# A four-stage transformer block on one core: expert products with gate and up weights stationary, and the order of the first attention units of layer 1

## The reference

```python
# experts: E=16, top 2, 128 hidden units each
p = sigmoid(x @ gate_w.T); p = p / sum(p)
w, idx = top_k(p, 2); w = w / sum(w)
gate, up = split(x @ gate_up_proj[e])        # [256, 2*128] for expert e
y_e = (silu(gate) * up) @ down_proj[e]       # [128, 256]
out = sum over the two chosen experts of w_e * y_e
# layer 1, per head: rope on q and k, alibi, 30*tanh(s/30), causal softmax, context, Wo
```

## Time and profile before

| | |
|---|---|
| median of 3 runs | 534.26 us (533.25 to 538.05) |
| profiled execution | 533.59 us |
| its span, first to last instruction | 531.1 us |
| mean granted TensorE clock | 0.974 |
| TensorE busy, the page | 497.8 us, 94% of the span |
| expert stage, first up record to last scatter | 221.1 to 275.8 us |

### The profile page before, as it was taken

How to read it: one execution, slowest core, us unless ns; L and a number is a source line. 1 busy time by engine, 2 the same in 40 slices (tenths; PEclk the granted TensorE clock), 3 DMA queues, 4 the chain that set the end, 5 groups by cost and what they waited for, 6 DMA issues and landing times.

```text
span 531.1 us, 10729 instructions
## 1 busy us (share of the span) xinstructions
PE 497.8 (94%) x3592; PEld 434.7 (82%) x3592; DVE 380.4 (72%) x833; ACT 339.7 (64%) x761; POOL 294.0 (55%) x289
## 2 busy tenths in 40 slices
PE   8999999999999996899958979999999999999994
PEld 7668888888888785688836869999999999999883
DVE  4798888888883275655537897779857985588556
ACT  5756777777766646344324776778766876676663
POOL 5757677767764136255551676776554664465330
PEclk9999999999999999899987988999999999999998
DMA  8939999940000672455564000000000000000001
GB/s 270 398 85 383 314 331 318 322 151 0 0 1 1 225 295 81 114 156 162 181 216 171 0 1 2 1 0 2 1 2 1 1 2 0 2 1 1 0 22 60
DMA packets 17756, 56.78 MB, mean 107 GB/s; under 512 B 2628, under 2 KB 12362, under 8 KB 15914
## 3 DMA queue, kind: packets, MB, share of 16 engines
q1 hardware_dynamic: 14960, 49.81, 27.5%
q0 software_dynamic: 2752, 6.40, 3.6%
HBM read 49.19 MB, written 28.45 MB: 146 GB/s over the span
## 4 chain that ended last, share of the span: by engine, by line
PE 78%; DVE 7%; ACT 5%; issue 3%; DMA 3%; POOL 2%; SPq 0%; DVEq 0%; POOLq 0%; ACTq 0%
PE bank L443 10%; PE bank L445 10%; PE bank L444 10%; PE bank L991 5%; PE bank L586 5%; PE bank L508 4%; PE bank L611 3%; PE bank L1008 3%; PE bank L588 2%; PE bank L735 2%; PE bank L720 2%; PE bank L722 2%; PE bank L721 2%; PE bank L622 2%; PE bank L702 2%
## 5 line engine op out<-in xcount | busy, mean ns | idle before, releaser
L1100 ACT ACTIVATE probs<-bank,neg_max,q_scale 128x256 f32<-128x256 f32 (+1 forms) x128 | 63.7, 507 | 39.1 <-DVE neg_max L1770 39.1
L1986 POOL TENSOR_TENSOR probs<-probs,inv_sum 128x512 f32<-128x512 f32 x64 | 51.5, 826 | 44.1 <-DVE inv_sum L1778 44.1
L2019 POOL TENSOR_TENSOR exps<-exps,tables 128x256 f32<-128x256 f32 x32 | 24.7, 771 | 75.2 <-ACT exps L1210 75.0
L1210 ACT ACTIVATE exps<-bank 128x768 f32<-128x768 f32 x32 | 25.9, 808 | 41.3 <-PE bank L702 41.3
L1590 DVE TENSOR_TENSOR q_lo<-q_sum,q_hi 128x512 fp32r<-128x512 f32 x32 | 28.8, 899 | 29.0 <-ACT q_hi L1164 28.6
L2006 POOL TENSOR_TENSOR swapped<-swapped,tables 128x512 f32<-128x512 f32 x32 | 43.4, 1359 | 5.2 <-ACT swapped L1131 5.1
L2115 POOL DMA_INDIRECT y_rows<-y_slot,dest x31 | 29.7, 959 | 30.0 <-issue 18.2
L1756 DVE TENSOR_TENSOR swapped<-bank,tables 32x512 f32<-32x512 f32 x64 | 44.4, 693 | 1.4
L1978 POOL TENSOR_TENSOR qT<-qT,swapped 128x512 f32<-128x512 f32 x32 | 40.8, 1274 | 6.1 <-DVE swapped L1756 6.1
L443 PE MATMUL bank<-x,wq_hi 128*128 128x256 f32 x128 | 38.6, 301 | 0.1
L586 PE MATMUL bank<-keysT,qT 128*128 128x256 f32 x128 | 38.2, 380 | 0.0
(11 more groups left out here) (281 smaller groups left out, 1766.6 us busy)
## 6 DMA issues: line engine op xcount, KB each, us to landing
slots<-in_c_unused SPq DMA_DIRECT2D x20, 1036.0 KB, 35.5
gu_all<-in_gate_up SPq DMA_DIRECT2D x4, 1024.0 KB, 7.8
xg<-slots SPq DMA_DIRECT2D x31, 129.5 KB, 2.2
wvo_raw<-in_wvo SPq DMA_DIRECT2D x1, 2560.0 KB, 18.4
dn_all<-in_down SPq DMA_DIRECT2D x1, 2048.0 KB, 7.7
wq_full<-in_Wq SPq DMA_DIRECT2D x1, 2048.0 KB, 17.8
wo_raw<-in_Wo SPq DMA_DIRECT2D x1, 2048.0 KB
wqk_raw<-in_wqk SPq DMA_DIRECT2D x1, 1536.0 KB, 9.9
```

Of the source, the lines that this page charges most:

```text
L1100: ins = act.activation(probs[:, par, h, c0:c1], bank[:, 2 * par + h, c0:c1], ACT.Exp, bias=neg_max[:, par, i:i + 1], scale=q_scale[:, b, t ...
L1986: ins = pool.tensor_tensor(some, some, inv, ALU.mult)
```

## The change

**Experts.** ScalarE gets a new step `take_weights(k)`: it reads the expert's number of block k into a register and copies that expert's 128 x 512 gate and up weights from `gu_all` to one of two fixed places (`GU = 2`) in `gu_block`. `up(k)` then takes these as the stationary operand and moves the block's 128 rows, in four matmuls of 128 columns, so that its result has hidden units on partitions, gate in columns 0 to 127 and up in 128 to 255. The product of silu and up is then already what `down` needs: `turn_act` and `copy_act` are gone, and the loops have one stage fewer. `gate_block(k)` writes `actT`, and `down(k-1)` follows `up(k)`. The first two `take_weights` stand ahead of ACT's first `copy_block`; later ones follow `silu`, two blocks ahead.

**Layer 1.** In units n = 1 to 3 DVE's `context_norm(n-1)` and (n = 2, 3) `context_lo(n-2)` follow `query_cos(n+3)` directly, ahead of `query_lo`, `keys_sum` and `query_sum`; in units n = 2 and 3 ACT's `context_hi` stands ahead of `act_query_hi` and exp. The two tiles of `normalise(1, 1)` are taken apart: the first stands at the head of unit 1, the second behind `query_lo(3)`.

```diff
@@ -273,7 +274,8 @@
     eps, minus_half = table_probe[:, 19:20], table_probe[:, 17:19]
     idx_f = x_rows[:, :, D:D + TOP]
     xT_f32 = q_sum
-    gated, act_tok = (swapped[:, i, 0:2 * FF].rearrange("p (i n) -> p i n", i=2) for i in range(2))
+    gu_block = q_sum[:].rearrange("p g (c f) -> p g c f", c=KD)
+    gated = swapped[:, 0, 0:2 * P].rearrange("p (i n) -> p i n", i=2)
     wk_hi, wk_lo = w_hi, w_lo
     slots = nc.dram_tensor("slots", (REGIONS * REGION, W), F32, kind="Internal").ap()
     y_rows = nc.dram_tensor("y_rows", (TOP * (B * T + KINDS * REGION), D), F32, kind="Internal").ap()
...
@@ -981,26 +980,22 @@
                 mm = pe.transpose(bank[:, turned(k), c * P:c * P + P], xg[:, k % XG, c * P:c * P + P], ident[:])
             mm.then_inc(mo["xgT_done"], 1)
 
-        def up(k, experts):
+        def up(k):
             pe.wait_ge(mo["xgT_copied"], k + 1)
+            pe.wait_ge(mo["gu_copied"], k + 1)
             if k >= 2:
                 pe.wait_ge(mo["act_ready"], k - 1)
-            for c in range(KD):
-                for i, e in enumerate(experts):
-                    rows = slice(ROWS * i, ROWS * i + ROWS)
-                    mm = pe.matmul(bank[rows, up_bank(k), 0:2 * FF], xgT[:, k % 2, c, rows],
-                                   gu_all[:, bass.ds(e, 1), c, :].rearrange("p e f -> p (e f)"),
-                                   start=c == 0, stop=c == KD - 1, skip_group_check=True)
+            for i in range(PER_STEP):
+                rows = slice(ROWS * i, ROWS * i + ROWS)
+                for half in range(2):
+                    dst = bank[:, up_bank(k), half * P + ROWS * i:half * P + ROWS * i + ROWS]
+                    for c in range(KD):
+                        mm = pe.matmul(dst, gu_block[:, k % GU, c, half * FF:half * FF + FF], xgT[:, k % 2, c, rows], start=c == 0, stop=c == KD - 1,
+                                       skip_group_check=True)
             mm.then_inc(mo["up_done"], 1)
 
-        def turn_act(k):
+        def down(k, experts):
             pe.wait_ge(mo["act_ready"], k + 1)
-            if k >= 2:
-                pe.wait_ge(mo["actT_copied"], k - 1)
-            pe.transpose(bank[:, actT_bank(k), 0:P], act_tok[:, k % 2, :], ident[:]).then_inc(mo["actT_done"], 1)
-
-        def down(k, experts):
-            pe.wait_ge(mo["actT_copied"], k + 1)
             if k >= 2:
                 pe.wait_ge(mo["y_copied"], k - 1)
             for i, e in enumerate(experts):
...
@@ -1016,18 +1011,16 @@
             pe.wait_ge(x_or_expert_in[j], 32)
         turn_block(0)
         experts_of = {}
-        for i in range(STEPS + 2):
+        for i in range(STEPS + 1):
             if i < STEPS:
                 experts_of[i] = [pe.value_load(block_expert[0:1, m:m + 1], min_val=0, max_val=E - 1)
                                  for m in range(PER_STEP * i, PER_STEP * i + PER_STEP)]
             if i + 1 < STEPS:
                 turn_block(i + 1)
             if i < STEPS:
-                up(i, experts_of[i])
-            if 1 <= i <= STEPS:
-                turn_act(i - 1)
-            if i >= 2:
-                down(i - 2, experts_of.pop(i - 2))
+                up(i)
+            if i >= 1:
+                down(i - 1, experts_of.pop(i - 1))
 
         pe.wait_ge(mo["y_copied"], STEPS)
         pe.wait_ge(y_back[0], 16)
...
@@ -1212,6 +1205,8 @@
                 act_swap_queries(act, n + 3)
             if n == 1:
                 act_swap_keys(act, 0, 1)
+            if 2 <= n < HEAD:
+                context_hi(n)
             if n + 2 < B * PAIRS:
                 act_query_hi(act, n + 2)
             if HEAD <= n < B * PAIRS - 3:
...
@@ -1223,7 +1218,7 @@
                 act.activation(exps[:, n % 2, :], exps[:, n % 2, :], ACT.Exp, scale=30.0).then_inc(at1["exp_done"], 1)
             if n == B * PAIRS:
                 load_table(act, 2 * B + 7, ACT.Sqrt)
-            if n >= 2 and not (b < B and n + 2 >= B * PAIRS):
+            if n >= HEAD and not (b < B and n + 2 >= B * PAIRS):
                 context_hi(n)
             if n == 0:
                 act.wait_ge(ld["wo1_in"], 16)
...
@@ -1366,21 +1361,35 @@
             act.activation(xgT[:, k % 2, :, :], bank[:, turned(k), 0:D].rearrange("p (c n) -> p c n", c=KD),
                            ACT.Copy).then_inc(mo["xgT_copied"], 1)
 
+        def take_weights(k):
+            e = act.value_load(block_expert[0:1, k:k + 1], min_val=0, max_val=E - 1)
+            if k >= GU:
+                act.wait_ge(mo["up_done"], k - GU + 1)
+            act.activation(gu_block[:, k % GU, :, :], gu_all[:, bass.ds(e, 1), :, :].rearrange("p e c f -> p (e c) f"),
+                           ACT.Copy).then_inc(mo["gu_copied"], 1)
+
         def silu(k):
             act.wait_ge(mo["up_done"], k + 1)
             if k >= 2:
                 act.wait_ge(mo["act_ready"], k - 1)
-            act.activation(gated[:, k % 2, :], bank[:, up_bank(k), 0:FF], ACT.Silu).then_inc(mo["silu_done"], 1)
+            act.activation(gated[:, k % 2, :], bank[:, up_bank(k), 0:P], ACT.Silu).then_inc(mo["silu_done"], 1)
 
         act.wait_ge(ld["wq1_in"], 16)
         act.wait_ge(ln["y_done"], NT)
         for i in range(PAIRS):
             act.activation(chunk(wq_hi, i), chunk(wq_full, i), ACT.Copy).then_inc(kv["w_hi"], 1)
+        act.wait_ge(mo["table_steps"], 4)
+        for j in range(4):
+            act.wait_ge(x_or_expert_in[j], 32)
+        take_weights(0)
+        take_weights(1)
         copy_block(0)
         for k in range(STEPS):
             if k + 1 < STEPS:
                 copy_block(k + 1)
             silu(k)
+            if k + 2 < STEPS:
+                take_weights(k + 2)
         load_table(act, 2 * B + 8, ACT.Sqrt)
         act_layer1(act)
 
...
@@ -1521,14 +1530,14 @@
                 dve.wait_ge(n3["z_read"], b + 1)
             dve_statistics(dve, counted, norm, b)
 
+        def normalise_second(t):
+
+            dve.wait_ge(ln["sqrt_done"], root_of(1, 1))
+            dve.tensor_scalar(x_tok[:, t, :], x_tok[:, t, :], moments[:, t, 0:1], inv_dev[:, 0, t:t + 1],
+                              ALU.subtract, ALU.mult).then_inc(ln["x_new"], 1)
+
         def normalise(norm, b):
-            if (norm, b) == (1, 1):
-                dve.wait_ge(ln["sqrt_done"], root_of(1, 1))
-                for t in (2, 3):
-                    dve.tensor_scalar(x_tok[:, t, :], x_tok[:, t, :], moments[:, t, 0:1], inv_dev[:, 0, t:t + 1],
-                                      ALU.subtract, ALU.mult).then_inc(ln["x_new"], 1)
-            else:
-                dve_normalise(dve, counted, norm, b)
+            dve_normalise(dve, counted, norm, b)
 
         def shift_of(b):
 
...
@@ -1643,23 +1652,29 @@
                 add_z(0)
             if n == 3 * PAIRS + 5:
                 add_z(1)
+            if n == 1:
+                normalise_second(2)
             if n < HEAD:
                 query_cos(n + 3)
+                if n >= 1:
+                    context_norm(n - 1)
+                if n >= 2:
+                    context_lo(n - 2)
             if n == 1:
-                context_norm(0)
                 keys_cos(0, 1)
-                normalise(1, 1)
             if n + 2 < B * PAIRS:
                 query_lo(n + 2)
+            if n == 1:
+                normalise_second(3)
             if n == 2:
                 keys_sum(0, 1)
             if HEAD <= n < B * PAIRS - 3:
                 query_cos(n + 3)
-            if 2 <= n < B * PAIRS + 1:
+            if HEAD <= n < B * PAIRS + 1:
                 context_norm(n - 1)
             if n + 3 < B * PAIRS:
                 query_sum(n + 3)
-            if n >= 2:
+            if n >= HEAD:
                 context_lo(n - 2)
             if n == 3:
                 keys_lo(0, 1)
...
@@ -1937,15 +1952,9 @@
         def gate_block(k):
             dve.wait_ge(mo["silu_done"], k + 1)
             if k >= 2:
-                dve.wait_ge(mo["actT_done"], k - 1)
-            dve.tensor_tensor(act_tok[:, k % 2, :], gated[:, k % 2, :], bank[:, up_bank(k), FF:2 * FF],
+                dve.wait_ge(mo["down_done"], k - 1)
+            dve.tensor_tensor(actT[:, k % 2, :], gated[:, k % 2, :], bank[:, up_bank(k), P:2 * P],
                               ALU.mult).then_inc(mo["act_ready"], 1)
-
-        def copy_act(k):
-            dve.wait_ge(mo["actT_done"], k + 1)
-            if k >= 2:
-                dve.wait_ge(mo["down_done"], k - 1)
-            dve.tensor_copy(actT[:, k % 2, :], bank[:, actT_bank(k), 0:P]).then_inc(mo["actT_copied"], 1)
 
         def copy_y(k):
             dve.wait_ge(mo["down_done"], k + 1)
...
@@ -1959,14 +1968,12 @@
                                      in1=xg[:, k % XG, D + 2:D + 3], op0=ALU.not_equal,
                                      op1=ALU.add).then_inc(mo["dest_ready"], 1)
 
-        for i in range(STEPS + 2):
-            if 1 <= i <= STEPS:
-                copy_act(i - 1)
+        for i in range(STEPS + 1):
             if i < STEPS:
```

(9 more changed lines are left out.)

## The result

The changed kernel took 540.54 us (median of 4 runs, 538.13 to 542.46), the kernel before 533.94 beside it (4 runs): a ratio of 1.0107, 95% interval 1.0067 to 1.0147, so slower by 5.7 us by that ratio, where I forecast 530.2. The execution that was profiled is the 542.46 (span 540.4), the longest of the four, so its distances are somewhat larger than those of the median run.

The account below looks back on a forecast made before the run. TensorE, busy 94% of the span, was taken as the bound. Experts -3.6 and layer 1 -0.5 give -4.1 us on the profiled 533.59: 529.5, and 530.2 as median (0.7 above); range 527.8 to 534.8.

Parts of the forecast that it names:

- The step that failed: Expert stage: TensorE's streaming alone bounds it, at 1.63 us a block; the other engines answer inside the block.
- rival (a): Expert stage: ScalarE's chain becomes the bound, 1.67 to 1.85 us a block, total 533.8 to 539.4; chance 0.14.
- 3.6 sooner: Expert stage in sum: -2.5 from shorter blocks, +0.1 at start-up, -1.2 in the tail, so -3.6 us.
- forecast 4.2: Expert stage's tail: last scatter 4.2 us after the last up product's start, where it was 5.41; 1.2 us sooner.
- block 1.55 (1.54): Expert stage: TensorE's block becomes 1.54 us, 0.09 less, with eight up records taking 0.89.
- the lower bound: Expert stage's best case, -4.4 us: up product at 0.85, all blocks, no start-up loss, plus the tail.
- context 1 without a wait: Layer 1: TensorE finds context 1 ready when queries(6) end, near 313, so its 3.2 us wait goes.
- query_lo(4) meets wo_lo: Layer 1: query_lo(4) instead of k_sum runs beside GpSimd's wo_lo, ending about 314.2; k_sum ends at 314.8.
- My list of signs: What would show the forecast; for layer 1: context 1's wait gone, another in its place, k_sum still stretched by GpSimd.
- The rule I quoted: Layer 1: a VectorE instruction with two SBUF inputs is blocked for the whole of a GpSimd instruction reading SBUF.
- -0.5: Layer 1: the wait moves from context 1 to scores(4); gain taken as 0.5 us, from -0.1 to -1.2.
- rival (b): Layer 1: the clock falls in the second pause, costing 1.4 to 3.4 us, total 531.6 to 533.6; chance 0.23.

Follow-up runs that it names:

- experiment 6: Changed kernel with GpSimd's scatter of y replaced by a plain DMA into consecutive rows: 533.55 us, ratio 0.9969 to the kernel before.
- kernel 9: Changed kernel with one more SyncE wait, for VectorE's copy of y of block k - 8, before loading block k: 533.09 us, ratio 0.9969 to the kernel before.
- kernel 2: Kernel before with only the new order of layer 1's first units, its expert blocks kept: 536.44 us, ratio 1.0038 to the kernel before.
- 4: Kernel before plus a ScalarE register read of each block's expert number, used for nothing: 535.66 us, ratio 1.0021 to the kernel before.

## Why the prediction was wrong

**The step that failed** is the reading of the expert stage: "nothing but PE's own streaming bounds the stage, and POOL, DVE and ACT answer inside it". I took that as true at 1.54 us because it was true at 1.63. The profile before shows no hold, so nothing in my sum had a place for one, and rival (a), the only one that ended slower, put the loss on ScalarE's chain. What came in its place: holds of 1 to 2 us between the end of TensorE's product and its semaphore update, for which the instruction behind it waits. They are absent in the one kernel with holds around it that has no scatters (6). In the profile after, the stage ends 5.8 us later, 1.1 of it from its later start, where I had 3.6 sooner. In kernel 9, without holds, the step is right: 1.55 a block, TensorE busy 39.65 of 40.

**The terms that held.** Kernel 9 is the changed kernel without holds, so it measures them. The end of its expert stage:

```profile
267.59 1.05 PE L993 MATMUL bank<-xgT,q_sum 128*128 128x128 f32 x8
...
271.76 0.96 POOL L2122 DMA_INDIRECT y_rows<-y_slot,dest  x1 [0.31 <-issue]
...
276.75 1.00 DVE L1515 SCALAR_TENSOR_TENSOR x_rows<-yg,p_top,x_rows 128x256 f32<-128x256 f32 x2 [6.17 <-DMA yg<-y_rows]
```

Last scatter 4.17 us after the last up product (forecast 4.2); up records 0.11 apart, block 1.55 (1.54); the first addition at 276.75, 3.3 sooner than the 280.06 before (forecast 3.6). One of my bounds was added up wrong: up records at their columns save 0.13 a block, 4.0 over 31 blocks and not 3.2, so the lower bound was -5.2 and not -4.4; nothing measured comes near it. ScalarE's copy takes 630 ns (613 taken) and its read costs TensorE nothing: rival (a) did not happen.

**Layer 1.** Right: context 1 without a wait, query_lo(4) meets wo_lo and ends near 314.2, k_sum near 314.8, keys_lo at 324.0, scores(4) then; all of it in the trace of kernel 2. My list of signs still had k_sum stretched, against the working; it takes 0.68. The rule I quoted held in its direction, as q_lo takes 1.71 beside GpSimd's wo_lo. Wrong was the choice between -0.5 and rival (b): scores(4) gained nothing, and the clock fell behind the second pause. That cost 1.55 us in kernel 2, within the 1.4 to 3.4 of the rival, and 2.7 in the profile after, where the clock is low from ahead of scores(4) on: 0.73 more from their start to their bias record, and 1.97 in the unit. I had it at 0.23; with two pauses in the place of one behind which the clock had fallen, it should have had the most weight.

**Where the clean stage's gain goes.** Kernel 9 is only 1.5 us faster than before: 533.09, which lies in rival (b)'s 531.6 to 533.6. It begins layer 1's scores 1.8 us sooner, not 3.3 (first before, then kernel 9):

```profile
296.31 0.39 PE L443 MATMUL bank<-q_hi,k_hi 128*128 128x512 f32 x1
```

```profile
294.47 0.39 PE L442 MATMUL bank<-q_hi,k_hi 128*128 128x512 f32 x1
```

The windows of TensorE behind its expert stage:

```profile
276.70:286.20 9.50, 8.18 (x36) 6.26 (x37) 7.61 (x22) 2.59 (x6) 0.10 (x1) 0.50 0.59 200
286.20:295.80 9.60, 9.60 (x67) 8.68 (x67) 6.89 (x9) 6.79 (x12) 3.48 (x3) 1.00 0.00 1
```

The clock is low until 286.1, that is 9.4 us of work behind the first addition; before, it was back at 284.92, 4.9 us behind it. So 1.5 us of what the stage saves are given back in slow matmuls, and 1.6 more in unit four: the scores behind it start at 331.36, where they started at 331.56 before. In the changed kernel it is the same: a second low stretch (292.75 to 296.16) makes +5.8 at the first addition +7.3 at the first scores.

**What stays open** is why the holds come. In the executions that have them they need the scatter, and they appear at 1.52 to 1.55 us a block in either form of the up product and at 1.66 in the new form, but not at 1.63 in the old form (2 and 4). Whether they appear at all in the new form goes with whether the trace has all its semaphore updates. That is a coincidence of two things in 20 traces, not a cause: the gaps begin ahead of the stage, in 2, 4 and 6 too, so the holds don't make them, but a third thing may make both. Every execution here, timed ones too, is a recorded one, so I can't exclude that the recording takes part. The Trainium skill, "NOTIFIC — the notification-queue block", section 7.1, describes a setting in which a full record queue stalls its engine; no run here shows whether that plays a part. The next runs would be the changed kernel without any recording, and a scatter spaced to some 1.6 us where there are holds; they weren't made.

## What to carry to other kernels

"The other engines answer inside the block" holds at the pace at which it was read; before a stage is made faster, look at what else runs every block beside TensorE (here a scatter of 0.96 us in GpSimd) and hold out a rival for it, with a price per block. When a kernel lacks an effect, repeat the unchanged kernel beside it before believing the cure, and look in the traces for a mark, in work that both share, that tells the two executions apart. And where an edit swaps one pause of TensorE for two, count the clock first: a pause removed is worth nothing if a later one still lets it fall into busy work.

## What the runs showed of the hardware

- A product's waiter can start 1.86 us after the end of the product's record while TensorE works on; the semaphore updates of four TensorE products came 0.47 to 1.83 us after their records' ends, all within 0.18 us (profile after), where they come within 0.02 in the kernel before.
- The same program ran at 533.09 and at 543.80 us on two chips on which the kernel before took 534.63 and 534.83; the first trace holds 256 of 256 semaphore updates of the routing scatter, the second 132.
- The scatter is GpSimd's for 0.96 us, while its data land 2.9 us after the issue (median in the profile of kernel 9). A plain DMA of the same bytes from the same queue holds GpSimd for 0.54 us (experiment 6).
